# Attention: the maxima of two heads side by side in halves of the array, over four banks

## The reference

```
attn  = einsum('bqhd,bkhd->bhqk', Q, K)     # 4 batches, 32 heads of 16, 640 tokens
probs = softmax(attn, axis=-1)
ctx   = einsum('bhqk,bkhd->bqhd', probs, V)
```

## Time and profile before

| | us |
|---|---|
| median of three runs (1658.5 to 1664.55) | 1659.09 |
| profiled execution, its own time | 1668.71 |
| its span in the trace | 1666.9 |
| TensorE busy | 1262.8 |
| VectorE busy | 1221.9 |
| ScalarE busy | 834.9 |
| GpSimd busy | 448.1 |

### The profile page before, as it was taken

One profiled execution on the slowest core, in us unless ns is written; L12 is line 12 of the kernel. 1 busy time (PEld: TensorE's weight loads), 2 busy tenths in 40 slices (PEclk: granted clock), 3 DMA queues, 4 the chain that ended last, 5 costly groups with the idle time before them and its releaser, 6 DMA issues. The chain is left out here.

```text
span 1666.9 us, 29887 instructions
## 1 busy us (share of the span) xinstructions
PE 1262.8 (76%) x10050; PEld 725.5 (44%) x10170; DVE 1221.9 (73%) x2038; ACT 834.9 (50%) x1748; POOL 448.1 (27%) x277
## 2 busy tenths in 40 slices
PE   0257247745989999999998898427629999999993
PEld 0245213211434444444443333105527777777772
DVE  7985999978877888888886888468665555555551
ACT  3674313320766777767776667763104444444441
POOL 4000306754133343333430021100012333333311
PEclk9988669975999999999999899757559999999997
DMA  5000205679366677776665473365249999999965
GB/s 160 0 1 1 92 0 186 215 230 200 118 181 180 184 197 202 206 198 180 194 170 119 86 162 117 88 120 158 95 144 353 312 310 310 310 312 312 309 199 145
DMA packets 115128, 294.09 MB, mean 176 GB/s; under 512 B 19986, under 2 KB 54802, under 8 KB 104656
## 3 DMA queue, kind: packets, MB, share of 16 engines
q1 hardware_dynamic: 90296, 209.27, 41.5%
q0 software_dynamic: 23712, 81.28, 18.2%
q10 hardware_dynamic: 1056, 2.79, 0.6%
HBM read 208.03 MB, written 90.32 MB: 179 GB/s over the span
## 5 line engine op out<-in xcount | busy, mean ns | idle before, releaser
L1478 ACT ACTIVATE pT<-p 128x512 f32<-128x512 f32 x800 | 422.0, 607 | 194.2 <-PE p L1369 109.4
L1441 DVE TENSOR_REDUCE mxa<-p 128x1 f32<-128x512 f32 x640 | 409.4, 682 | 107.5 <-PE p L1351 107.3
L1351 PE MATMUL p<-ks,qs 96*128 96x512 bf16 x640 | 254.7, 401 | 51.9 <-DMA vs<-d_v 31.3
L1369 PE MATMUL p<-qs,ks 128*128 128x512 bf16 x560 | 216.7, 387 | 31.6 <-DMA qs<-nmT 20.9
L1387 PE MATMUL p<-pT,vs 128*32 128x128 f32 (+1 forms) x2560 | 207.2, 442 | 1.4 <-ACT pT L1478 1.4
L2103 POOL DMA_INDIRECT d_acc<-yo,slot_row x47 | 74.6, 1588 | 267.7 <-DVE yo L2251 255.6
L2133 PE MATMUL p<-x,w 128*128 128x256 bf16 (+1 forms) x1728 | 145.5, 246 | 0.0
L2133 PEld LDWEIGHTS p<-x,w 128*128 128x128 bf16 x1728 | 133.5, 98 | 13.9
L1387 PEld LDWEIGHTS p<-pT,vs 128*32 128x32 f32 x2560 | 67.1, 109 | 153.9 <-issue 109.3
L1351 PEld LDWEIGHTS p<-ks,qs 96*128 96x128 bf16 x640 | 62.3, 98 | 155.1 <-DVE mxa L1441 58.5
L1319 POOL CAST xT<-xT 128x2048 bf16<-128x2048 f32 x24 | 45.3, 1887 | 304.8 <-PE p L1387 292.3
(11 more groups left out here) (406 smaller groups left out, 2073.0 us busy)
## 6 DMA issues: line engine op xcount, KB each, us to landing
w<-d_w SPq DMA_DIRECT2D x18, 2048.0 KB, 9.6
d_w<-xT POOLq DMA_DIRECT2D x24, 1024.0 KB, 6.3
shared<-d_w SPq DMA_DIRECT2D x10, 2048.0 KB, 7.8
w<-d_w SPq DMA_DIRECT2D x18, 1024.0 KB, 10.7
xT<-in_w1T POOLq DMA_DIRECT2D x16, 1024.0 KB, 10.6
qs<-d_q SPq DMA_DIRECT2D x192, 80.0 KB, 3.6
ks<-d_k SPq DMA_DIRECT2D x192, 80.0 KB, 3.8
d_v<-xT SPq DMA_DIRECT2D x20, 512.0 KB, 4.4
```

Source lines behind the costliest of these rows:

```text
L1351: mm = pe.matmul(out, qs[u][0:STACK, h, q], ks[u][0:STACK, h, 0:512], start=True, stop=True)
L1369: mm = pe.matmul(out, ks[u][:, h, k], qs[u][:, h, 0:512], start=True, stop=True)
L1441: dve.tensor_reduce(mxa[u][:, h, qt:qt + 1], bank, AX.X, ALU.max, negate=True).then_inc(s_mfree, 1)
L1478: act.activation(dst, ps[:, second_bank(c, s)], ACT.Exp).then_inc(s_p, 1)
```

## The change

The four heads of a group are taken as two pairs, head j with head j + 2. The stacks are laid out anew: rows 0 to 47 and rows 64 to 111, with zeros between them. Heads 0 and 1 have their three main products (main by main, main by middle, middle by main) in the lower half and the three fine ones in the upper half; heads 2 and 3 the other way round. The row for the maximum is now row 112. A first-pass unit of 512 keys is now a pair: two matmuls of 48 rows, one in each half of the array, into two banks that lie next to each other, and they use the main products alone. The maximum that is subtracted is therefore that of approximate scores for these keys, which cancels between numerator and sum. The unit of the last 128 keys uses the whole stack, as the second pass does. One reduction covers both banks of a pair.

The banks are dealt out as two pairs for the first pass and two single ones for the second. A group's first pass has 16 units now (ten pairs, five units of the rest, the turn, which is slot 2), `LEAD` is 10, and a list of widths (2 for a pair, 1 for the others) spreads them over the 25 second-pass units. A load has 24 transfers of 40 KB and the values. Four fillings prepare each stack pair instead of two, and the third part of each first load waits for them.

```diff
-    M1 = U2 + 1
-    TURN = 4
-    STACK, MROW = 6 * HD, 6 * HD
-    PARTS = [(0, 0), (0, 1), (0, 2), (1, 0), (1, 1), (2, 0)]
-    LOADS = 2 * len(PARTS) + 1
+    PAIR = GH // 2
+    UNITS_QT = PAIR + 1
+    TURN = PAIR
+    M1 = UNITS_QT * KT + 1
+    WIDTH = [1 if m == TURN or (m - (m > TURN)) % UNITS_QT == PAIR else 2 for m in range(M1)]
+    HALF = P // 2
+    MROW = HALF + 3 * HD
+    MAIN = [(0, 0), (0, 1), (1, 0)]
+    FINE = [(0, 2), (1, 1), (2, 0)]
+    LOADS = 4 * (len(MAIN) + len(FINE)) + 1
-    LEAD = 16
+    LEAD = 3 * UNITS_QT + 1
+    LAST_TURN = 13
-        mbank, sbank = [0, 1, 2], [3, 4, 5]
+        mbank, sbank = [0, 2], [4, 5]
...
             for u in which:
-                eng.memset(qs[u][STACK:P], 0.0).then_inc(done, 1)
-                eng.memset(ks[u][STACK:P], 1.0).then_inc(done, 1)
+                for at in (HALF // 2, HALF + HALF // 2):
+                    eng.memset(qs[u][at:at + HALF // 2], 0.0).then_inc(done, 1)
+                    eng.memset(ks[u][at:at + HALF // 2], 0.0 if at < HALF else 1.0).then_inc(done, 1)
...
-                for at, (q_part, k_part) in enumerate(PARTS):
-                    part_rows = slice(at * HD, (at + 1) * HD)
-                    for dst, src, part in ((qs, d_q, q_part), (ks, d_k, k_part)):
...
+                for at in range(len(MAIN)):
+                    if first and at == len(MAIN) - 1:
+                        sp.wait_ge(s_setv if u < 2 else s_setg, SETS * (u % 2 + 1))
+                    for pair in range(2):
+                        heads = slice(PAIR * pair, PAIR * (pair + 1))
+                        for half in range(2):
+                            q_part, k_part = (MAIN if half == pair else FINE)[at]
+                            part_rows = slice(half * HALF + at * HD, half * HALF + (at + 1) * HD)
+                            for dst, src, part in ((qs, d_q, q_part), (ks, d_k, k_part)):
...
-                qt, h = divmod(slot - (slot > TURN), U1)
+                qt, j = divmod(slot - (slot > TURN), UNITS_QT)
                 q = slice(qt * P, (qt + 1) * P)
-                if h < GH:
-                    mm = pe.matmul(out, qs[u][0:STACK, h, q], ks[u][0:STACK, h, 0:512], start=True, stop=True)
+                if j < PAIR:
+                    for half in range(2):
+                        rows, h = slice(half * HALF, half * HALF + len(MAIN) * HD), PAIR * half + j
+                        mm = pe.matmul(ps[:, first_bank(c, slot) + half], qs[u][rows, h, q], ks[u][rows, h, 0:512],
+                                       start=True, stop=True, tile_position=(half * HALF, 0))
...
+                begins = [sum(WIDTH[slot] for _, slot in ahead[:k]) * U2 // sum(WIDTH) for k in range(len(ahead))]
                 for s in range(U2):
-                    for cc, slot in ahead[s * M1 // U2:(s + 1) * M1 // U2]:
-                        first_pass(i, cc, slot)
-                    if following == 1 and s == M1 - LEAD + 3:
+                    for k, (cc, slot) in enumerate(ahead):
+                        if begins[k] == s:
+                            first_pass(i, cc, slot)
+                    if following == 1 and s == LAST_TURN:
...
-            pe.wait_ge(s_setv, 4)
-            pe.wait_ge(s_setg, 4)
+            pe.wait_ge(s_setv, 2 * SETS)
+            pe.wait_ge(s_setg, 2 * SETS)
...
-                    if h < GH:
-                        dve.tensor_reduce(mxa[u][:, h, qt:qt + 1], bank, AX.X, ALU.max, negate=True).then_inc(s_mfree, 1)
+                    if j < PAIR:
+                        pair = ps[:, first_bank(c, slot):first_bank(c, slot) + 2]
+                        dve.tensor_reduce(mxa[u][:, j::PAIR, qt], pair, AX.X, ALU.max, negate=True).then_inc(s_mfree, 1)
```

More of the change, by code:

```diff
@@ L1222, in set_stacks, with first_bank @@
             for u in which:
-                eng.memset(qs[u][STACK:P], 0.0).then_inc(done, 1)
-                eng.memset(ks[u][STACK:P], 1.0).then_inc(done, 1)
-        def first_bank(c, s):
-            return mbank[(s + M1 * (c % R)) % len(mbank)]
+                for at in (HALF // 2, HALF + HALF // 2):
+                    eng.memset(qs[u][at:at + HALF // 2], 0.0).then_inc(done, 1)
+                    eng.memset(ks[u][at:at + HALF // 2], 0.0 if at < HALF else 1.0).then_inc(done, 1)
+        def first_bank(c, m):
+            return mbank[(m + M1 * (c % R)) % len(mbank)]
+        SETS = 4
         def second_bank(c, s):
@@ L1238, in _, with load @@
         def _(sp):
-            def load(i, c):
+            def load(i, c, first=False):
                 n, u = num(i, c), c % R
                 rows = n * (GH * HD)
-                for at, (q_part, k_part) in enumerate(PARTS):
-                    part_rows = slice(at * HD, (at + 1) * HD)
-                    for dst, src, part in ((qs, d_q, q_part), (ks, d_k, k_part)):
-                        sp.dma_start(dst[u][part_rows].rearrange("p h t -> p (h t)"),
-                                     src[part, bass.ds(rows, GH * HD)].rearrange("(c h) t -> c (h t)", h=GH)
-                                     ).then_inc(s_ld[u], 16)
+                for at in range(len(MAIN)):
[7 more added lines that the diff above has]
+                            for dst, src, part in ((qs, d_q, q_part), (ks, d_k, k_part)):
+                                sp.dma_start(dst[u][part_rows, heads],
+                                             src[part, bass.ds(rows, GH * HD)].rearrange("(c h) t -> c h t", h=GH)[:, heads]
+                                             ).then_inc(s_ld[u], 16)
                 sp.dma_start(vs[u][:], d_v[bass.ds(n, 1)].rearrange("o p k c -> p (o k) c")).then_inc(s_ld[u], 16)
@@ L1257, in _ @@
             for c in range(R):
-                load(0, c)
+                load(0, c, first=True)
             def step(i, c):
@@ L1347, in first_pass @@
                     pe.wait_ge(s_ld[u], 16 * LOADS * (i + c // R + 1))
-                qt, h = divmod(slot - (slot > TURN), U1)
+                qt, j = divmod(slot - (slot > TURN), UNITS_QT)
                 q = slice(qt * P, (qt + 1) * P)
-                if h < GH:
-                    mm = pe.matmul(out, qs[u][0:STACK, h, q], ks[u][0:STACK, h, 0:512], start=True, stop=True)
+                if j < PAIR:
[3 more added lines that the diff above has]
+                                       start=True, stop=True, tile_position=(half * HALF, 0))
                 else:
                     for h in range(GH):
-                        mm = pe.matmul(out[:, h * REST:(h + 1) * REST], qs[u][0:STACK, h, q], ks[u][0:STACK, h, 512:T],
+                        mm = pe.matmul(out[:, h * REST:(h + 1) * REST], qs[u][0:MROW, h, q], ks[u][0:MROW, h, 512:T],
                                        start=True, stop=True)
```

## The result

The changed kernel takes 1719.0 us (median of four runs, 1712.1 to 1728.1), the kernel before 1660.9 in the same series. The ratio is 1.035, with a 95% interval of 1.030 to 1.041: slower, by 58 us where 61 were forecast. The profiled execution of after has a span of 1717.6 us.

The account below looks back on a forecast made before the run. A ring bounds each group: first score unit to issue of the maxima's transfer, then its landing. 29 groups at 1.5 us (43.5), group 0 1.5, last two 2.9 and 2.5, start 5.7, sums 5.5: 61.6 us, giving 1720, range 1684 to 1757.

Parts of the forecast that it names:

- The score banks: Second-pass score loop with two banks instead of three: five units take 3.67 us where 3.10 stood, issue at 13.7 us.
- the base: Group period in the kernel before, taken as 18.90 us between two first score units; forecast 20.4, 1.5 more.
- The loads: 24 half-size transfers inside the groups: 1.6 us of cover, taken as nothing, up to 2 us a group without cover.
- The pairs: First-pass pairs in row halves of the array: 0.44 us each taken, bounds 0.22 and 0.65; 0.14 us a group.
- VectorE: Joint reductions over two banks save nothing to 2 us of a group's 15.8 on VectorE, worth nothing in time.
- Start, sums and tail: Ends of attention: start +5.7 us, wait for the sums' transfer +5.5, last group 2.9 and the one ahead 2.5.
- The scale: Profiled execution 1668.7 us plus 61.6 gives 1730.3; the runs' median lies 0.58% lower, so 1720.
- (a): Rival: TensorE, not the score loop, bounds the groups; pairs save 0.22 us each, 17.4 a group, 1627 us; chance 0.07.
- (b): Rival: the maxima's transfer lands early, so 19.5 us a group and 1694 us; chance 0.14.
- (c): Rival: the pairs' halves do not run together and each switch drains; 20.9 us a group, 1735 us; chance 0.12.
- (d): Rival: loads or the maxima's transfer come a microsecond later; 21.4 us a group, 1750 us; chance 0.06.

## Why the prediction was right or wrong

**The score banks** were right in mechanism. The score ring alone, at the end of attention in the kernel after, takes 3.75 us for five units (1095.99 to 1099.74) where 3.67 were worked out:

```profile
1095.99 1.28 PE L1405 MATMUL p<-pT,vs 128*32 128x512 f32 x16
...
1098.29 0.88 PE L1387 MATMUL p<-qs,ks 128*128 128x512 bf16 x2 [0.47 <-ACT pT L1499]
1099.42 0.39 PE L1387 MATMUL p<-qs,ks 128*128 128x512 bf16 x1 [0.26 <-ACT pT L1499]
1099.74 1.28 PE L1405 MATMUL p<-pT,vs 128*32 128x512 f32 x16
```

From first unit to issue it forecast 13.7 us and 13.85 came; for a group in which the transfer is early it gave some 19.5 us, and the last three of the 24 groups, at whose end TensorE does not wait for it, take 19.7 to 19.8. What it mis-sized is the base: 18.90 us was one good group. The 24 groups of the kernel before average 466.1 / 24 = 19.4, because some of them wait longer for the transfer (3.29 us in the earlier trace rows). With two banks alone those waits are largely covered (6.7 us of waiting for the transfer from 400 to 1000 us, where the kernel before has 24.2), so the banks cost 1.08 us a group, not 1.4.

**The loads** were taken as nothing inside the groups ("up to 2 us a group" was left open, for another reason). That is the step that failed. It looked for the harm at the first pair that needs a load, with 1.6 us of cover; that cover held, no pair waits for a load in the loop. The harm came by way of the maxima's transfer, which the prediction held at 6.62 us. It landed after 7.0 in the mean and cost the clock three times; with the banks' 26 us of the 24 groups' 35 known from the run of its own, 9 are left, and the run with 12 transfers gives 8 of them, in one profiled execution each. The two misses nearly cancel: 35 against 36 forecast. That is luck. In the kernel before, the same cut of the loads costs 64 us. The sum came out right partly because the new stack rows soften what this step overlooked.

**The pairs** cost 0.43 us between score units (0.65 less one product of 0.22); 0.44 was taken. The bounds held, and so did it that a pair gains nothing among whole-array products.

**VectorE** worth nothing: right. Two joint reductions in a row take 2.35 us where four single ones took 2.47; so even its own time is hardly less.

```profile
718.70 2.35 DVE L1462 TENSOR_REDUCE mxa<-p 128x2 f32<-128x1024 f32 x2
```

**Start, sums and tail**: +6.7, +5.8 and +4.5 us against 7.2, 7.0 and 5.4. The sums' own wait grew by 4.0 us, not 5.5.

**The scale**: attention grew by 56.1 us, the span by 50.7; what lies outside attention was 5 us shorter in that one execution. The medians say +58.

**The rivals.** (a) TensorE is no bound: two score banks alone are slower by 2.4%. (b) The transfer did not come early; 6.17 us was the shortest of the 16 landings that TensorE waited for, and only after GpSimd's last fetch of weights did two units of the 18 find it there (within 5.9 us). (c) The halves do overlap, and both sides drain: half of it is true, and it does not show in the time, since whole-array pairs cost the same. (d) came in part. It was given 0.06. Two score banks with 24 transfers into rows 0 to 95 took 1745 us, where it said 1750; it is the new rows that kept the changed kernel from it.

## What to carry to other kernels

Before a bank is taken from a loop, count the ring through it; here two score banks instead of three cost 38 us, and what was bought with them saved nothing in the loop: a change of the array's layout on both sides of every pair costs the product that the pair saves, and two joint reductions take hardly less than four single ones (2.35 us and 2.47). When transfers are cut smaller, look not only at who needs them but at every small transfer that a ring waits for while they run, and issue that one early: one constant was worth 14 us here and 54 with the smaller loads. Take a loop's base from the mean of many groups, not from one clean one.

## What the runs showed of the hardware

- 24 transfers of 40 KB instead of 12 of 80 KB made a 5 KB transfer on another queue land 8.34 us after its issue instead of 6.70, as long as GpSimd moved weights too; other target rows brought 8.62 down to 7.63.
- A wait of 2.94 us was followed by a granted clock of 0.66 over four microseconds, and the lost time moved the next issue by 1.5 us. So a late transfer is paid twice.
- Two matmuls in row halves last together as long as one (0.39 us), and cost 0.1 us more on each side among whole-array products.
- A small VectorE operation can stand as long as a large one of GpSimd. In order of time, first in a group of the loop with GpSimd's subtraction beside it, then in one where GpSimd does nothing, then in the group of 26.4 us in the table's fourth stretch:

```profile
909.20 4.08 POOL L1336 TENSOR_TENSOR xT<-xT 128x2048 bf16<-128x2048 f32 x1
912.63 0.67 DVE L1467 TENSOR_TENSOR nm<-mxa,mxb 128x20 f32<-128x20 f32 x1
...
932.39 0.18 DVE L1467 TENSOR_TENSOR nm<-mxa,mxb 128x20 f32<-128x20 f32 x1
...
1028.17 5.59 POOL L1343 TENSOR_TENSOR xT<-xT,shared 128x2560 f32<-128x2560 f32 x1 [114.02 <-DMA shared<-d_sum]
1028.88 4.92 DVE L1467 TENSOR_TENSOR nm<-mxa,mxb 128x20 f32<-128x20 f32 x1
```

Alone it takes 0.18 us. Wherever one of GpSimd's two-operand operations runs beside it in the kernel after, 24 times, it ends 0.03 to 0.04 us after that one, here after 0.67 and 4.92 us. The Trainium skill (SBUF — State Buffer, SBUF: two separate sides) names it: a VectorE operation with two SBUF inputs and a GpSimd operation that reads SBUF share a pair of ports, and who comes second waits for the whole instruction; the trace agrees.
